# Writing the zeros of the result table at the start of the program, and moving two batches' normalising from GpSimd to ScalarE

## The reference, cut to what matters

```
x = x + attn_a(layernorm(x))          # causal, 16 heads, query and key normalised, rotary on half of the heads
x = x + ffn(layernorm(x))             # 64 experts, the best 4 for each row, and a shared expert
x = x + attn_b(layernorm(x))          # not causal
x = x + ffn(layernorm(x))

ffn: logits = flat @ router_w;  the 4 largest of logits + bias for each row
     comb   = their softmax scores, divided by their sum
     routed = sum over the 4 of comb * (silu(flat @ wg[e]) * (flat @ wu[e])) @ wd[e]
     shared = two always active experts
```

## Time and profile before

| | us |
|---|---|
| median of 3 runs | 1092.6 (1087.54 to 1094.36) |
| profiled execution, its own time | 1090.27 |
| profiled execution, span | 1088.7 |
| busy: PE, PEld | 898.7 (83%), 644.0 (59%) |
| busy: DVE, POOL, ACT | 704.9 (65%), 488.1 (45%), 475.1 (44%) |
| TensorE clock granted, mean | 0.914 |

### The profile page before, as it was taken

The page is one execution under the profiler, slowest core; times in us unless marked ns, Lnnn a source line. Parts: engine busy times, 40 slices in busy tenths (PEclk is TensorE's granted clock), DMA queues, the critical chain, the costliest instruction groups (busy, mean ns, idle before and its releaser), DMA issues.

```text
span 1088.7 us, 23319 instructions
## 1 busy us (share of the span) xinstructions
PE 898.7 (83%) x7194; PEld 644.0 (59%) x7194; DVE 704.9 (65%) x2286; ACT 475.1 (44%) x994; POOL 488.1 (45%) x625
## 2 busy tenths in 40 slices
PE   6995999998896979996876799998584699998761
PEld 5773666664454867874665355547353477786551
DVE  6888898867951546554565799948892165544553
ACT  3653565561101545553564488873210255553000
POOL 3001254436775423316773344311777533333775
PEclk9997999998897999998997699999698699999896
DMA  8387999909998899854479877501944599873443
GB/s 273 60 154 130 190 253 243 268 24 276 273 245 224 245 288 296 252 162 120 126 166 187 140 114 114 81 2 28 305 142 144 177 298 297 262 235 114 125 124 111
DMA packets 159161, 197.83 MB, mean 182 GB/s; under 512 B 17376, under 2 KB 137696, under 8 KB 155872
## 3 DMA queue, kind: packets, MB, share of 16 engines
q1 hardware_dynamic: 118688, 111.40, 45.2%
q0 software_dynamic: 22848, 68.18, 20.2%
q10 hardware_dynamic: 17504, 16.78, 4.7%
HBM read 132.86 MB, written 90.18 MB: 205 GB/s over the span
## 4 chain that ended last, share of the span: by engine, by line
PE 41%; POOL 15%; DVE 15%; DMA 13%; issue 9%; SPq 4%; ACT 3%; DVEq 0%; POOLq 0%; ACTq 0%
POOL xd L555 9%; PE ps L973 9%; PE ps L742 5%; PE ps L985 5%; PE ps L639 5%; PE ps L956 4%; DMA yd<-tmp 4%; PE ps L727 4%; POOL spill L596 4%; DMA spill<-yd,slot 3%; DMA spill<-in_we 1%; POOL tables L596 1%; DMA tables<-yd,slot 1%; PE ps L769 1%; ACT tmp L1015 1%
## 5 line engine op out<-in xcount | busy, mean ns | idle before, releaser
L1015 ACT ACTIVATE tmp<-ps 128x256 f32<-128x256 f32 (+1 forms) x344 | 156.5, 477 | 129.0 <-PE ps L956 72.8
L1161 ACT ACTIVATE tmp<-ps 128x384 f32<-128x384 f32 (+1 forms) x256 | 135.0, 544 | 61.1 <-PE ps L730 37.9
L555 POOL DMA_INDIRECT xd<-big,slot x128 | 126.7, 989 | 61.3 <-issue 52.1
L493 POOL COPY arena<-negmax 24x2048 bf16<-24x2048 bf16 x32 | 60.5, 1890 | 133.8 <-ACT negmax L1015 91.7
L639 PE MATMUL ps<-arena 96*128 96x256 bf16 (+1 forms) x512 | 98.3, 279 | 16.0 <-DVE tmp L1391 6.9
L596 POOL DMA_INDIRECT spill<-yd,slot x96 | 96.2, 1002 | 32.2 <-issue 18.6
L727 PE MATMUL ps<-arena 120*128 120x256 bf16 (+1 forms) x512 | 101.2, 265 | 0.5 <-ACT tmp L1161 0.2
L1758 DVE SCALAR_TENSOR_TENSOR tmp<-tmp,ps 128x128 f32<-128x128 f32 x128 | 36.7, 287 | 94.8 <-ACT tmp L1246 94.1
L956 PE MATMUL ps<-ident,big 128*128 128x128 f32 x512 | 74.2, 289 | 28.2 <-issue 27.2
L1394 DVE TENSOR_REDUCE tmp<-ps 128x2 f32<-128x512 f32 x128 | 81.8, 684 | 11.6 <-PE ps L639 11.4
L1768 DVE COPY tmp<-ps 128x256 f32<-128x256 f32 x128 | 52.2, 423 | 56.1 <-PE ps L985 29.8
(11 more groups left out here) (203 smaller groups left out, 1854.7 us busy)
## 6 DMA issues: line engine op xcount, KB each, us to landing
big<-xd POOLq DMA_DIRECT2D x128, 256.0 KB, 4.6
arena<-parts SPq DMA_DIRECT2D x192, 128.0 KB, 5.6
xd<-zero SPq DMA_DIRECT2D x8, 2048.0 KB, 13.9
spill<-in_we SPq DMA_DIRECT2D x128, 128.0 KB, 3.2
yd<-tmp POOLq DMA_DIRECT2D x64, 256.0 KB, 3.3
yd<-tmp ACTq DMA_DIRECT2D x64, 256.0 KB, 3.8
arena<-in_we SPq DMA_DIRECT2D x14, 1024.0 KB, 6.5
yd<-zero SPq DMA_DIRECT2D x8, 1024.0 KB, 23.4
```

The source lines that it names most:

```text
L555: pool.indirect_dma_start(xd[:, :], bass.IndirectOffsetOnAxis(ap=slot[:, i, k:k + 1], axis=0), xn_all[:, i, :], None).then_inc(scattered.s ...
L1015: return act.activation(dst, src, ACT.Copy)
L1161: act.activation(prob[h % 8][:, 0:n], ps[2 + h % 2][:, 0:n], ACT.Exp).then_inc(exp_ready.sem, 1)
```

## The change

1. The eight transfers that write the zeros of the upper half of `yd` move in SyncE's order from behind `load_fixed` of block 0 to a place right behind the loads of the inputs, ahead of the marker's copies and of all `store_parts`. They write from the upper 64 partitions of `zero`, as before.
2. `BY_ACT[0]` goes from 8 to 6: for batches 6 and 7 of block 0 GpSimd computes only the power and the shift, and ScalarE normalises the rows. VectorE computes one negated mean more for each of the two (`variance`). For batch 6 GpSimd's part stays where it was, and ScalarE's follows 8 heads into the last step of the attention. For batch 7 GpSimd's part moves from between tiles 1 and 2 of the scatter to between tiles 3 and 4, and ScalarE's stands between `keep_turned(6)` and `keep_turned(7)`.

```diff
-BY_ACT = (8, 0)
+BY_ACT = (6, 0)
...
             sp.wait_ge(setup_done.sem, 2)
+            for b in range(B):
+                n = NTILE // B
+                sp.dma_start(yd.rearrange("(p a) d -> p a d", a=NTILE)[64:, b * n:b * n + n, :],
+                             zero[64:, :].rearrange("p (a d) -> p a d", a=1).broadcast_to([64, n, D])).then_inc(y_zeroed.sem, 16)
...
                 for g in range(FSLOTS):
                     load_fixed(sp, g)
-                if r == 0:
-                    for b in range(B):
-                        n = NTILE // B
-                        sp.dma_start(yd.rearrange("(p a) d -> p a d", a=NTILE)[64:, b * n:b * n + n, :],
-                                     zero[64:, :].rearrange("p (a d) -> p a d", a=1).broadcast_to([64, n, D])).then_inc(y_zeroed.sem, 16)
...
                 for i in range(NT):
-                    if r == 0 and i == TB:
-                        normal_rows(B - 1)
+                    if r == 0 and i == 2 * TB:
+                        root_rows(B - 1)
...
                             keep_turned(h)
+                        if s == B + 1 and h == 8 and r == 0:
+                            send_rows(6)
...
                 keep_turned(6)
+                if r == 0:
+                    send_rows(7)
                 keep_turned(7)
```

## The result

The changed kernel takes 1107.84 us (median of 5 runs, 1104.84 to 1114.65) against 1092.39 (5 runs, 1086.84 to 1094.36): ratio 1.0176, 95% interval 1.0146 to 1.0206. The quotient of the two medians is 1.0141, a little outside that interval; with five runs of each the size of the loss is no better known than that. The profiled execution is the slowest of the five, 1114.65 us with a span of 1113.1. The other four spans lie between 1103.3 and 1108.0, so differences at a place in the trace are read here rather than the difference of the two spans.

The account below looks back on a forecast made before the run. Bound: GpSimd's scatter, and in the projection TensorE, VectorE and ScalarE handing work round. Stall 21.4 plus clock 3.0 less 8.1 won gave 16.3 us over 1090.3, 1106.6; the median lies 2.3 higher: 1108.9, range 1097 to 1118.

Parts of the forecast that it names:

- The rate of the zeros and the stall: Projection: zeros from 64 partitions take 41 us, batch 0's store lands at 70.7, ScalarE's `first_part` of batch 2 stalls 21.4 us.
- The prediction's line between gain and loss: Zeros at the start: within some 27 us (310 GB/s), stall and clock would equal the 8.1 us won.
- Nothing absorbs it: Behind the projection's stall: ScalarE, VectorE and TensorE all stop, and the 21.4 us delay goes to the end.
- The rival of a partly absorbed stop: Projection: TensorE and VectorE run ahead, the stage takes 5 to 10 us back; 1099 to 1104, chance 0.09.
- the hidden: Start: zeros take 21.8 us in an empty queue, the stall is 2.2 us; 1086.7, chance 0.13.
- the 138 GB/s cases: Start: the zeros keep 138 GB/s alone, take 61 us and stall 41 us; 1129, chance 0.03.
- The clock after the stop: Projection: TensorE restarts at half clock for some 7 us and loses 3 us, bounds 0 and 4.
- The scatter: Block 0: moving GpSimd's work for batch 7 wins 3.44 less 1.4, 2.0 us, bounds 1.5 and 2.3.
- The last landing: Block 0, last scatter to first table load: 7.65 us becomes block 1's 3.08, so 4.57 us won.
- The rival of no gain at the scatter: End of scatter: the last landing stays 7.65 us, only 2 us won; 1115, chance 0.05.
- The clock at the expert loop: Start of the expert loop: less TensorE idleness keeps the clock up, 1.5 us won, bounds 0 and 2.
- What comes behind: After the projection's stall: nothing is tied to a time, so the delay goes unchanged to the end.

Follow-up runs that it names:

- wide_at_start: Changed kernel with the same zeros at the same place, but read from all 128 partitions: 1089.70 us, ratio 0.9978 to the kernel before.
- half_at_start: Changed kernel with four of the eight zero transfers at the start, four behind `load_fixed`: 1159.42 us on the slower third chip, ratio 0.9945 to the kernel before.
- zeros_only: Changed kernel with `BY_ACT[0]` back at 8, so only the zeros move and GpSimd normalises batches 6 and 7: 1112.46 us, ratio 1.0177.
- hole_gpsimd_rows_again: As hole_again, but GpSimd normalises batches 6 and 7 as in the kernel before: 1089.14 us, ratio 0.9967 to the kernel before.
- hole_again: Repeat of wide_in_the_hole beside two relatives, on another chip: 1085.55 us, ratio 0.9939 to the kernel before.
- act_rows_only: Kernel before with only ScalarE normalising batches 6 and 7, the zeros at their old place: 1093.42 us, ratio 1.0024.
- wide_in_the_hole: Changed kernel with zeros from 128 partitions, issued behind clearing the first two batches' part of `xd`: 1086.27 us, ratio 0.9937 to the kernel before.
- narrow_in_the_hole_again: As hole_again, but the zeros are read from 64 partitions: 1085.43 us, ratio 0.9941 to the kernel before.

## Why the prediction held, step by step

The forecast was 16.3 us more and 1108.9; the medians differ by 15.45. The mechanism is the one forecast, and three terms of the sum are off. That the total is so close is luck in part: the stall came out 0.8 us longer than forecast, the clock behind it 2.0 cheaper and the gain at the scatter 1.0 smaller, and the three errors cancel. What the profiled execution loses behind that stays out of the sum (below).

**The rate of the zeros and the stall** were right. Forecast 200 to 205 GB/s and a store that lands at 70.7; measured 193 and 71.57, a stall of 71.57 - 49.33 = 22.2 us for the 21.4 forecast. wide_at_start and half_at_start show that it hangs on the length of the transfers: 3.41 us of waiting at 384 GB/s, none with half the bytes. The prediction's line between gain and loss, zeros within 27 us, leaves out its own 3 us for the clock; with them it is 24.7.

**Nothing absorbs it**, as forecast. TensorE's rotations are 22.1 and 23.1 us late and the first scatter 273.45 - 250.19 = 23.3. The rival of a partly absorbed stop is out, and the hidden and the 138 GB/s cases with it.

**The clock after the stop** was mis-sized: 3 us forecast, 23.1 - 22.1 = 1.0 measured. The granted clock was 0.50 as forecast, but not "for some 7 us". TensorE starts again at 77.90 and is busy almost without a gap; the granted clock is 0.50 until 80, 0.64 from 80 to 81 and 1.00 from 81 on. Only the rotation (2.07 us for 1.12) and the turning behind it (1.06 for 0.60) pay, 1.4 us, and 0.3 come back since TensorE no longer waits 0.28 us for VectorE before the next rotation. In zeros_only the same restart costs more. Its rotations are 22.4 and 24.6 us late, so 2.2 are lost, and the window shows the clock at 0.50 to the end:

```profile
80.00:84.00 4.00, 4.00 (x18) 2.40 (x17) 3.17 (x4) 2.02 (x3) 0.00 (x0) 0.50 0.88 145
```

Why the clock came back some 3 us later in one execution than in the other stays open.

**The scatter** was mis-sized too. Both gaps are as forecast (0.49 and 1.91 us), but from the first to the last issue GpSimd takes 360.23 - 273.45 = 86.78 us against 337.50 - 250.19 = 87.31: 0.5 won and not 2.0. Most of the missing part is in the scatters themselves, which in these four traces take longer when `normal_rows(7)` doesn't stand between them. Groups of instructions of GpSimd in the scatter, kernel before, after, hole_gpsimd_rows_again and hole_again:

```profile
L555 POOL DMA_INDIRECT xd<-big,slot x64 | 62.7, 980 | 27.4 <-issue 23.2 <-POOL pause_at L455 3.9 <-POOL big L503 0.3
```
```profile
L554 POOL DMA_INDIRECT xd<-big,slot x64 | 64.2, 1004 | 29.8 <-issue 25.6 <-POOL pause_at L454 3.9 <-ACT big L1135 0.3
```
```profile
L554 POOL DMA_INDIRECT xd<-big,slot x64 | 62.7, 980 | 27.4 <-issue 23.2 <-POOL pause_at L454 3.9 <-POOL big L502 0.3
```
```profile
L554 POOL DMA_INDIRECT xd<-big,slot x64 | 64.1, 1002 | 29.8 <-issue 25.9 <-POOL pause_at L454 3.9
```

64 scatters take 62.7 us with the pause and 64.1 to 64.2 without it: 1.4 to 1.5 us go back. The other traces of these two chips narrow that: zeros_only, with the pause, has 62.9, and act_rows_only, wide_at_start and wide_in_the_hole, without it, 63.6 to 63.7. So 0.7 to 1.5 us go back, and GpSimd wins 0.5 to 1.3. A few single scatters are long then, as 1.58 us at 284.24 above. That `normal_rows(7)` is the cause is argued from this pairing only; why those scatters, I can't say.

**The last landing** was right: 4.57 us won forecast, 7.65 - 3.11 = 4.54 measured. The rival of no gain at the scatter is out. act_rows_only, with the zeros beside the scatter and a landing of 8.89 us, shows that the zeros were the cause. The landing is 3.1 in every trace of the two chips with the zeros elsewhere and ScalarE's rows, but 3.82 in zeros_only and 4.34 in hole_gpsimd_rows_again, where GpSimd normalises. So in these traces the absence of the zeros alone gives 3.3 to 3.8 of the 4.54, and the rest comes only together with ScalarE's rows. The forecast took its 3.08 from block 1, where no zeros are written and ScalarE normalises, and so counted both without saying so the earlier trace rows.

**The clock at the expert loop** gave more: 1.5 us forecast, about 2.0 measured. The first turning is 366.51 - 348.29 = 18.2 us late, the second 372.68 - 356.49 = 16.2. The loads of the table are 18.2 late as well, so the 2.0 are the clock's. So 23.3 - 16.2 = 7.1 us were won by then, for the 8.1 forecast: 0.5 + 4.5 + 2.0, up to rounding.

**What comes behind** is looser than forecast ("nothing afterwards is tied to a time"). One profiled execution of each kernel, less the times of the kernel before, at TensorE's first turning of the expert loop (348.29), at its first group of 16 in the projection of block 1 (515.01), at GpSimd's first load of block 1 (851.08), and at the end of the span (1088.7):

| kernel | 348.29 | 515.01 | 851.08 | 1088.7 | median of runs |
|---|---|---|---|---|---|
| after | +18.2 | +19.0 | +20.0 | +24.4 | +15.45 |
| zeros_only | +21.5 | +21.8 | +20.5 | +23.9 | +20.9 |
| act_rows_only | -0.9 | -0.8 | -1.7 | +2.2 | +1.9 |
| wide_at_start | -2.9 | -0.2 | -0.6 | -0.4 | -1.9 |
| wide_in_the_hole | -6.3 | -6.1 | -6.8 | -3.5 | -5.3 |
| hole_again | -4.0 | -1.3 | -1.8 | -2.8 | -5.8 |
| hole_gpsimd_rows_again | -3.0 | -3.2 | -4.4 | -3.5 | -2.2 |
| narrow_in_the_hole_again | -4.6 | -4.2 | -6.3 | -5.3 | -5.9 |

The expert loops and gathers take some us more or less from one execution to the next: hole_again gives back 2.7 us in the first loop, wide_in_the_hole, the same kernel on another chip, 0.2. Of the 2.7, 1.6 are lost by the end of the second turning, while its clock is low. In the chain of waits the results' stores (`yd<-tmp`) show long stalls, here the first ones of the kernel after:

```profile
392.79 9.02 DMA yd<-tmp
...
412.24 9.82 DMA yd<-tmp
...
430.88 11.13 DMA yd<-tmp
```

In the trace of before there are two long ones in this loop, at 395.47 (10.62 us) and 416.32 (7.76), and one of 7.09 us by a load of weights (`spill<-in_we`, at 383.15). The sums, 29.97 and 25.47 us, differ by 4.5, and the loop loses 19.0 - 16.2 = 2.8, so the stalls are where the time goes, but don't add up to it. So of the 24.4 us of the profiled pair 16 to 18 are there by the first expert loop, and 6 to 8 come behind it; that those aren't of the change is argued from the spread of the runs and not shown. How the transfers of the expert loop fall together in one run or another stays open; no experiment here took it apart.

## What to carry to other kernels

Before moving a transfer into a quiet stretch, divide its bytes by the rate that its own source allows (a row of the same shape on full engines), and set the sum against the first consumer of anything that goes through the DMA engines behind it, on any queue: here 43 us of zeros went into 13 us of quiet. Another queue is no way round a full engine when the other queue's packets are eight times as long. And an improvement off the path shows nothing until the wait that covers it is gone: beside the zeros GpSimd's 1.3 us, won by ScalarE's rows, went whole into the longer landing (8.89 us for 7.65). What those rows are worth without the zeros, perhaps 3 us, the runs hardly tell from nothing.

## What the runs showed that I had not expected

- Two queues share the DMA engines by packets and not by bytes: 788 packets of 3.8 KB and 786 of 0.5 KB in 16 us. The long-packet queue had 94.0% of the time.
- With a pause of 3.4 us among 64 scatters these were 0.7 to 1.5 us shorter in sum (980 to 983 ns each against 993 to 1004), on the two chips without the long stops.
- Whether TensorE's clock falls at the start of the expert loop is not settled by the change: it stayed full with 0.23 us of idleness in the kernel after, and fell in hole_again with 3.25 us, as the windows of that kernel show; the groups of 16 there took 1.98 us as in the trace of before.

```profile
338.00:342.00 4.00, 3.01 (x14) 2.29 (x13) 0.69 (x1) 0.00 (x0) 1.78 (x3) 1.00 0.19 66
342.00:346.00 4.00, 1.11 (x6) 0.74 (x7) 0.00 (x0) 0.60 (x1) 2.88 (x4) 0.82 0.64 195
346.00:350.00 4.00, 3.17 (x14) 2.04 (x15) 0.00 (x0) 1.26 (x3) 2.53 (x5) 0.50 0.84 251
```

- One chip ran the same program 6% slower (1161.99 us before), with stops of 9 to 19 us of three engines at once in and before the shared expert, which no trace of the other chips shows. What they are stays open.
